# VectorE takes the first convolution's sums straight from PSUM, in a kernel of four residual layers

## What is computed

```python
x = x + grouped_conv(x, L0_weight)  + (cond @ L0_c_weight.T)[:, :, None] + fside[None, :, None]
x = x + einsum('boi,bih->boh', einsum('bk,koi->boi', att1, L1_weight), x) + (att1 @ L1_bias_k)[:, :, None]
x = x + grouped_conv(x, L2_weight)  + (cond @ L2_c_weight.T)[:, :, None] + fside[None, :, None]
x = x + einsum('boi,bih->boh', einsum('bk,koi->boi', att3, L3_weight), x) + (att3 @ L3_bias_k)[:, :, None]
```

## Time and profile before

| | |
|---|---|
| time, median of 3 runs | 2475.89 us (2475.6 to 2477.11) |
| the profiled execution | 2476.58 us |
| its span | 2474.8 us |
| PE busy | 2456.0 us, 99% |
| DVE busy | 2117.3 us, 86% |
| ACT busy | 1519.9 us, 61% |
| DMA | 357 MB, 144 GB/s over the span |
| ScalarE's copies of the sums, both convolutions (L657, L659, L673) | 129.6 + 129.6 + 235.6 us |
| VectorE's additions (L838, L840) | 288.7 + 288.7 us |
| VectorE's differences (L754) | 975.9 us of x, 568.7 us of x2 |

### The profile page before, as it was taken

The page is one execution under the profiler, slowest core; times in us unless marked ns, Lnnn a source line. Parts: engine busy times, 40 slices in busy tenths (PEclk is TensorE's granted clock), DMA queues, the critical chain, the costliest instruction groups (busy, mean ns, idle before and its releaser), DMA issues.

```text
span 2474.8 us, 99123 instructions
## 1 busy us (share of the span) xinstructions
PE 2456.0 (99%) x45256; PEld 1472.7 (60%) x45256; DVE 2117.3 (86%) x806; ACT 1519.9 (61%) x1120; POOL 23.3 (1%) x28
## 2 busy tenths in 40 slices
PE   8999999999999999999999999999999999999998
PEld 4444444455555555566666666666666666666665
DVE  7988988988988889889889888898898898888984
ACT  6666666666666656666666666666666666666665
POOL 3000000000000000000000000000000000000000
PEclk9999999999999999999999999999999999999999
DMA  9644444444444444444444444444444444444433
GB/s 348 208 128 127 157 140 127 141 151 132 127 145 152 127 127 158 138 127 143 150 131 127 146 150 127 129 157 138 127 144 150 130 127 149 148 127 129 159 104 121
DMA packets 186683, 357.24 MB, mean 144 GB/s; under 512 B 12754, under 2 KB 143834, under 8 KB 154010
## 3 DMA queue, kind: packets, MB, share of 16 engines
q1 hardware_dynamic: 186056, 354.60, 45.8%
q10 hardware_dynamic: 594, 2.13, 0.2%
HBM read 205.69 MB, written 150.99 MB: 144 GB/s over the span
## 4 chain that ended last, share of the span: by engine, by line
PE 98%; DVE 1%; ACT 1%; DMA 0%; issue 0%; SPq 0%; DVEq 0%; ACTq 0%
PE psum L410 62%; PE psum L481 35%; PE psum L379 0%; DMA out<-outb 0%; DMA diff<-expert_rows 0%; ACT shared L629 0%; DVE diff L759 0%; ACT diff L629 0%; DVE y L797 0%; DVE y L813 0%; DVE y L816 0%; ACT y L657 0%; ACT outb L680 0%; DVE h L789 0%; ACT y L629 0%
## 5 line engine op out<-in xcount | busy, mean ns | idle before, releaser
L410 PE MATMUL psum<-diff,prod_w 32*64 32x512 f32 x28672 | 1689.2, 587 | 2.2 <-issue 1.0
L410 PEld LDWEIGHTS psum<-diff,prod_w 32*64 32x64 f32 x28672 | 952.4, 131 | 629.7 <-issue 304.9
L754 DVE TENSOR_TENSOR diff<-xin 128x2052 f32<-128x2052 f32 x256 | 975.9, 3903 | 307.5 <-PE psum L410 307.5
L481 PE MATMUL psum<-y,mixw 32*64 32x512 f32 x16384 | 1028.7, 588 | 1.9 <-DVE y L816 1.9
L481 PEld LDWEIGHTS psum<-y,mixw 32*64 32x64 f32 x16384 | 575.3, 131 | 341.7 <-issue 186.5
L754 DVE TENSOR_TENSOR diff<-x 128x2055 f32<-128x2055 f32 x255 | 568.7, 2301 | 0.0
L720 ACT ACTIVATE x<-psum,bias_now 128x2048 f32<-128x2048 f32 x128 | 251.7, 1966 | 198.3 <-PE psum L481 198.3
L680 ACT ACTIVATE outb<-psum,bias_now 128x2048 f32<-128x2048 f32 x128 | 251.0, 1961 | 195.3 <-PE psum L481 193.8
L645 ACT COPY shared<-psum 128x2048 f32<-128x2048 f32 x128 | 238.8, 1866 | 171.8 <-PE psum L410 171.8
L838 DVE TENSOR_TENSOR y<-y,shared 128x2048 f32<-128x2048 f32 x126 | 288.7, 2291 | 15.6 <-ACT y L659 15.6
L673 ACT COPY y<-psum 128x2048 f32<-128x2048 f32 x126 | 235.6, 1870 | 91.8 <-PE psum L410 91.8
(11 more groups left out here) (80 smaller groups left out, 104.2 us busy)
## 6 DMA issues: line engine op xcount, KB each, us to landing
xin<-x SPq DMA_DIRECT2D x128, 1024.0 KB, 7.0
out<-outb SPq DMA_DIRECT2D x127, 1024.0 KB, 4.8
mixw<-mix_dram SPq DMA_DIRECT2D x512, 128.0 KB, 5.4
mix_dram<-shared SPq DMA_DIRECT2D x6, 1024.0 KB, 12.9
mix_dram<-y SPq DMA_DIRECT2D x6, 1024.0 KB, 10.7
mix_dram<-diff SPq DMA_DIRECT2D x2, 1024.0 KB, 12.0
mix_dram<-outb SPq DMA_DIRECT2D x2, 1024.0 KB, 13.9
y<-experts ACTq DMA_DIRECT2D x2, 512.0 KB, 4.3
```

The source lines that it names most:

```text
L410: return pe.matmul(psum[cols, half, g, :], prod_w[v][at, kind, s, cols], moving, start=start, stop=stop, skip_group_check=True)
L481: mm = pe.matmul(psum[cols, half, r, :], mixw[home][at, b, g, cols], y[home][at, :, g, b, :], start=g == 0, stop=g == GROUPS - 1)
L754: nc.vector.tensor_tensor(into(kind), in0, in1, op).then_inc(diff_ready[v], 1)
```

## The change

For the first convolution (v=0) ScalarE no longer copies the sums to y: take_sums returns behind the copies to shared. In `outputs`, VectorE takes the sums itself, from PSUM: it subtracts shared B from the sum in A in two parts of 1024 elements (behind conv_done[0] 5 and 6), adds shared A to the sum in B in one of 2048 (behind 8), writes y, and raises sums_taken[0] with each. In pair 0 the last one is in two parts. In VectorE's order the first convolution's additions now stand ahead of the ONLY_ODD difference of x2; the explicit wait for conv_done[0] 4 goes. y_ready is left for the second convolution alone, and who waited for y of the first waits for sums_taken[0]. The second convolution is as before.

```diff
+        def y_there(v, n):
+            return (sums_taken[0], COPIES * n + COPIES) if v == 0 else (y_ready, 2 * n + 2)
...
                 if parts:
-                    pe.wait_ge(y_part, 2)
+                    pe.wait_ge(sums_taken[0], 1)
+                    pe.wait_ge(y_part, 1)
                 else:
-                    pe.wait_ge(y_ready[m], 2 * n + 2)
+                    pe.wait_ge(*y_there(m, n))
...
                 nc.scalar.copy(shared[v][:, 1, 2:4], psum[:, B_HALF, 2:4, :]).then_inc(shared_ready[v], 1)
+                if v == 0:
+                    return
...
                 dve.wait_ge(shared_ready[v], COPIES * n + 3)
+                if v == 0:
+                    first = whole(n) and n == 0
+                    if first:
+                        for j in LAST_IN_Y[0]:
+                            dve.wait_ge(agg_stored[j], 16)
+                    lead, trail = slice(0, GROUPS // 2), slice(GROUPS // 2, GROUPS)
+
+                    def add(half, parity, at, op):
+                        return nc.vector.tensor_tensor(
+                            y[0][:, parity].rearrange("p g b m -> p g (b m)")[:, at], psum[:, half, at, :],
+                            shared[0][:, 1 - parity, at], op)
+
+                    dve.wait_ge(conv_done[0], CONV_SIGNALS * n + 5)
+                    add(A, 0, lead, ALU.subtract).then_inc(sums_taken[0], 1)
+                    dve.wait_ge(conv_done[0], CONV_SIGNALS * n + 6)
+                    add(A, 0, trail, ALU.subtract).then_inc(sums_taken[0], 1)
+                    if first:
+                        dve.wait_ge(conv_done[0], 7)
+                        add(B_HALF, 1, lead, ALU.add).then_inc(y_part, 1)
+                    dve.wait_ge(conv_done[0], CONV_SIGNALS * n + 8)
+                    add(B_HALF, 1, trail if first else slice(0, GROUPS), ALU.add).then_inc(sums_taken[0], 1)
                     return
...
                     diff_of_x2(i - 1, (ONLY_EVEN,))
-                    if has_front(i):
-                        dve.wait_ge(conv_done[0], CONV_SIGNALS * i + 4)
-                    diff_of_x2(i - 1, (ONLY_ODD,))
                 if has_front(i):
                     outputs(0, i)
+                if has_middle(i) and not (whole(i) and i == PAIRS):
+                    diff_of_x2(i - 1, (ONLY_ODD,))
```

## The result

The changed kernel takes 2514.12 us (median of 4 runs, 2513.88 to 2515.38), the kernel before 2476.26 us beside it: a ratio of 1.0154, 95% interval 1.0136 to 1.0171. That is 38 us slower, where 42 were forecast.

The account below looks back on a forecast made before the run. TensorE was taken to fill every 37.79 us turn, so its waits add: 61 turns x 0.65 = 39.7 us plus 2.5 in the first pairs, +42.2, gives a median of 2518 us; 8-in-10 range 2500 to 2543.

Parts of the forecast that it names:

- The bound: Loop: TensorE fills the whole 37.79 us turn; work taken off ScalarE or VectorE shortens nothing, each TensorE wait adds.
- Step 1: Second mix's start: VectorE's first addition to half A comes late, behind three x2 differences; 0.45 us lost a turn.
- step 3: Addition to half B: 2.29 us where ScalarE's copy took 1.87; leading row tiles lose 0.15 us more a turn.
- Step 2: Second addition to half A ends after the trailing row tiles need it; they lose another 0.17 us a turn.
- The first pairs: Ahead of the 61 turns: second convolution 1.2 us late, next pair's mix 1.3 us; together +2.5 us.
- the start-up's gain: First pair: additions start at the signals, not behind copies, so the mix starts 1.3 us earlier; not kept.
- ScalarE's relief at nothing: Loop: three ScalarE copies go in each pair, about 4 us a turn less busy, with no time saved.
- the hidden part: Rest of a turn: ONLY_ODD behind the additions ends at 1247.3, wanted at 1254.8; VectorE's idle stretch a little under 5 us.
- Dearer reads from PSUM: Rival: each of VectorE's three additions 0.066 us longer from PSUM; 0.78 us a turn, 2526 us; chance 0.12.
- A cover for the waits: Rival: TensorE's queued work covers the loop's waits, so not slower, 2473.5 to 2476 us; chance 0.09.
- The clock did not fall: Rival: short stops lower TensorE's granted clock in each turn, about 1.7 us a turn, 2620 us; chance 0.04.
- The third rival: Loop: only the first addition's lateness costs, partly got back by denser work; 0.25 us a turn, 2494 us; chance 0.07.

Follow-up runs that it names:

- the order alone: Kernel before, ScalarE still copying the sums, with the ONLY_ODD difference moved behind the first convolution's additions: 2477.26 us, ratio 1.0002.
- the one with both edits: Changed kernel with ONLY_EVEN also behind the additions and the 2048-element addition to half B in two of 1024: 2477.13 us, ratio 1.0002.
- the last: Changed kernel with ONLY_EVEN behind the additions, half B in two parts and pair 1 in an order of its own: 2477.21 us, ratio 1.0004.
- step 3 taken away: Changed kernel with the addition to half B in two parts, the order as in the change: 2512.36 us, ratio 1.0146.
- the run with VectorE earlier: Changed kernel with the ONLY_EVEN difference of x2 moved behind the additions too: 2484.80 us, ratio 1.0035.
- the run with one difference later: Changed kernel with the ONLY_ODD difference back ahead of the additions, as in the kernel before: 2676.03 us, ratio 1.0805.

## Why the prediction was right, and where its sizes were off

**The bound.** A turn of 37.79 us that TensorE fills: right. The kernel before and the three experiments without late additions (the order alone, the one with both edits, the last) have that turn to 0.01 us, and none is under it.

**Step 1**, 0.45 us forecast. VectorE's chain from its idle stretch to the first addition took 18.44 us where I had 18.56 (1240.26 less 1221.70), and the release took 0.15 us where I had 0.05 (the addition took 1.25 and not 1.22, ends at 1223.84, weights at 1223.96, matmul at 1223.99). The two offset: the mix starts 19.84 behind the end of the idle stretch, against 19.83 forecast and 19.38 before, so 0.46 us. (The leading tiles alone lost 0.38 there, 1223.61 against 1223.99; step 3 had left them 0.08 behind the trailing ones, whose signal ends VectorE's idle stretch: 0.57 from 1204.15 to 1204.72 where the kernel before has 0.49.) The low price of a release came from the start-up, where both records begin together.

**Steps 2 and 3**, 0.17 and 0.15 us forecast, 0.62 together with step 1 if the tiles keep their own delays, 0.77 if not. It is the first: 0.1 us for both, measured from the leading tiles' start to the next end of the idle stretch, and 0.1 with step 3 taken away. Alone, step 3 costs 0.14 (the run with VectorE earlier). I took 0.65 a turn between the readings; 0.547 was measured. This is the term that was too large: 61 x 0.65 = 39.7 stood for 59 turns and the last, 33.4. The trailing tiles show where it was. Step 2 was right: from their start in the mix to the next end of the idle stretch it is 18.31 us before (1241.18 to 1221.70 + 37.79) and 18.48 in the change (1224.02 to 1242.50), 0.17 more. But step 1 cost them 0.39 and not 0.45, as they start 19.48 us behind the end of the idle stretch before and 19.87 in the change: the forecast let them start 0.10 behind the leading ones, as before, and behind a stop the two start 0.03 apart.

**The first pairs**, 2.5 us forecast, 4.85 measured at the first point. VectorE was released from the start-up as worked out: four additions of 1.13 us each, 47.85 to 52.5, next differences on the landing of x at 54.04 (forecast 53.4), x2 differences at 68.73 (forecast 68.0), second convolution at 77.94 (forecast 77.0). Of that last 0.9 us, 0.6 is a late x, and the rest adds up on the way. What was left out is the clock: the start-up no longer has the slow stretch (1.00 from 56 to 58, where it was 0.50), but TensorE, early by the start-up's gain, stops for 5.09 us in pair 1 and then runs at 0.50. I had seen the mechanism at 54 and had not carried it to the stop that my own working made at 77. It is not the whole of the 4.85, though. Against the kernel before, the second convolution starts 2.13 us late (75.81 to 77.94; forecast 1.2), the mix behind it 3.16 (88.28 to 91.44), so the slow stretch costs 1.03 net, the second mix's stop adds 1.32 (forecast 1.3), and the last 0.37 comes between there and the first point.

The errors, +2.4 us in the first pairs, -6.3 in the turns, and +0.5 behind the last point, sum to -3.4 against the forecast span of 42.2 more. That the total came out closer than the turns did is luck: two errors of opposite sign.

**ScalarE's relief at nothing, and the hidden part.** Right: 243 us less busy, no effect. ONLY_ODD behind the additions costs nothing. VectorE's idle stretch is 5.3 us, where 5.1 was measured before and a little under 5 was forecast; the turn is longer and VectorE's work in it is not (32.81 us against 32.72).

**The rivals.** Dearer reads from PSUM: 1262 ns in the mean for 1024 elements here, but 1218 in the run with ONLY_EVEN behind and half B in two parts, and 2292 for 2048 from either memory. Additions of 2048 from SBUF alone grew as well in the change, to 2324 ns (line 844 above) from 2292, and did so in that run too (2326). So it is not the source of the data that makes 1262. Nor is it that additions stand alone: four in a row in the order of the change took 1266. What does, beside the place of the additions, stays open. The Trainium skill ("VectorE: DVE Perf Modes", section "The TRN2 errata — SBUF-src ops pay a fixed extra latency per instruction") has 62 cycles between the two sources; these runs don't show them. The rule of the Trainium skill on the port shared with GpSimd ("SBUF — State Buffer", "Who interferes with whom") agrees: the last of the four additions was 1.22 us long with a GpSimd instruction on two tensors beside it, where one with both inputs in SBUF had been 2.28 long beside such an instruction. A cover for the waits was not there, and nothing was got back behind a stop: 0.46 us was paid in full, and so were 1.13 and 2.2 us more. The clock did not fall in the loop of the change; it fell in pair 1, and in the run with one difference later it fell in a quarter of the turns, at stops of 2.3 to 2.5 us. The third rival, a part of step 1 got back by denser work, is out by the same runs.

## What to carry to other kernels

Where one engine fills the loop without a gap, the busy shares of the others say nothing on a change; each hand-over back to the full engine has a slack of its own, and an engine that is 86% busy can be late for one of them and idle 5 us elsewhere in the same turn. Before work is moved to an engine, follow its chain from its last idle stretch to the place of the new instruction: here that sum gave the first stop within 0.01 us, though by luck, as two errors of 0.1 us in it cancelled. A faster start-up can come back as a longer stop further on, and a stop of TensorE is to be priced with the clock behind it.

## What the runs showed of the hardware

The granted clock stood at 0.50 behind a stop of 5.09 us in pair 1 (24 records in 78 to 80, where 2 us at full clock hold 37), behind one of 2.71 us ahead of the second mix of pair 0 (0.50 in 112 to 114), and behind 15 of 59 stops of 2.3 to 2.5 us in the loop, from the stop's end for about 3 us, at 1.5 us each. At the other 44, of the same lengths and longer, and at stops of 1.2 to 1.5 us in each of 61 turns it stood at 1.00. The leading and the trailing row tiles of TensorE run on with delays of their own: a lag of 0.21 us made by one wait was still 0.17 half a turn later, and the larger of two delays counted in the turn, not their sum (38.34 us with step 3 and without it).
